# Self-attention key scores without mask matmuls: GpSimd zeroes the unseen exponentials, two score steps are interleaved, value products run two groups behind

## The reference

```python
w = jnp.einsum('bhqd,bhkd->bhqk', q, k) / jnp.sqrt(jnp.asarray(HD, q.dtype))
neg = jnp.finfo(w.dtype).min
if causal_bool:                       # self attention
    mask = jnp.tril(jnp.ones((ql, kl), bool))
    w = jnp.where(mask[None, None], w, neg)
if tril_diag2_additive:               # cross attention
    cm = jnp.tril(jnp.ones((ql, kl), w.dtype), k=2)
    w = w + jnp.where(cm == 0, neg, jnp.zeros((), w.dtype))[None, None]
w = jax.nn.softmax(w, axis=-1)
return jnp.einsum('bhqk,bhkd->bhqd', w, v)
```

## Time and profile before

| | |
|---|---|
| Median of three runs | 1644.99 us |
| Profiled execution | 1647.01 us, its span 1645.3 us |
| PE matmuls busy | 1434.1 us (87%) |
| DVE busy | 1116.3 us (68%) |
| ACT busy | 987.8 us (60%) |
| GpSimd (POOL) busy | 317.8 us (19%) |
| Self phases with both kinds of scores | 16, first to last step 19.58 us in most of them |
| Cross phases with both kinds | 14, first to last step 22.08 to 23.37 us in most of them |

### The profile page before, as it was taken

How to read it: one execution, slowest core, us unless ns; L and a number is a source line. 1 busy time by engine, 2 the same in 40 slices (tenths; PEclk the granted TensorE clock), 3 DMA queues, 4 the chain that set the end, 5 groups by cost and what they waited for, 6 DMA issues and landing times. The chain is left out here.

```text
span 1645.3 us, 39092 instructions
## 1 busy us (share of the span) xinstructions
PE 1434.1 (87%) x15448; PEld 877.4 (53%) x15448; DVE 1116.3 (68%) x3252; ACT 987.8 (60%) x1618; POOL 317.8 (19%) x428
## 2 busy tenths in 40 slices
PE   2667789989898989989898998989899898989887
PEld 1445564655555565655556465555646565555443
DVE  5557676767777776776777676677767667647344
ACT  2255675766757576675757576575757666571642
...
GB/s 69 57 77 52 55 22 55 21 44 38 22 59 9 67 15 39 36 32 50 10 72 10 50 26 39 43 16 64 10 56 20 44 32 28 9 24 12 15 5 9
DMA packets 79214, 58.05 MB, mean 35 GB/s; under 512 B 11004, under 2 KB 78902, under 8 KB 79030
## 3 DMA queue, kind: packets, MB, share of 16 engines
...
...
## 5 line engine op out<-in xcount | busy, mean ns | idle before, releaser
L1025 DVE TENSOR_REDUCE chunkmax<-ps 128x3 f32<-128x384 f32 (+1 forms) x1024 | 508.6, 553 | 119.2 <-PE ps L1379 113.6
L711 ACT ACTIVATE probs<-ps 128x768 f32<-128x768 f32 (+1 forms) x512 | 406.0, 809 | 199.3 <-PE ps L1374 195.5
L1444 PE MATMUL ps<-zT,w 128*128 128x512 f32 x576 | 281.0, 602 | 6.5 <-ACT silu_a L728 4.8
L728 ACT ACTIVATE silu_a<-ps,b 128x512 f32<-128x512 f32 x144 | 98.7, 685 | 197.9 <-PE ps L1444 174.5
L1359 PE MATMUL ps<-k_op,q_op 48*128 48x256 bf16 x512 | 147.4, 290 | 64.4 <-DVE chunkmax L1025 50.8
L1166 DVE SCALAR_TENSOR_TENSOR h_open<-ps,b,silu_a 128x512 f32<-128x512 f32 x128 | 95.8, 749 | 123.6 <-PE ps L1444 111.3
L1444 PEld LDWEIGHTS ps<-zT,w 128*128 128x128 f32 x576 | 102.8, 191 | 114.6 <-issue 87.4
L1341 PE MATMUL ps<-q_op,k_op 51*128 51x256 bf16 x512 | 141.7, 277 | 25.2 <-POOL lower L499 9.3
L1480 PE MATMUL ps<-hT,w 128*128 128x512 f32 x288 | 149.3, 599 | 3.8 <-DVE hT L1172 3.0
L1359 PE MATMUL ps<-xk_op,xq_op 51*128 51x256 bf16 x512 | 143.5, 282 | 6.1 <-DVE chunkmax L1025 5.7
L1371 PE MATMUL ps<-mask_q_lo,ident_lo 64*128 64x256 bf16 x512 | 145.9, 288 | 0.0
...
## 6 DMA issues: line engine op xcount, KB each, us to landing
q_op<-q_parts SPq DMA_DIRECT2D x192, 64.0 KB
xq_op<-xq_parts SPq DMA_DIRECT2D x192, 64.0 KB
...
```

The source lines that it names most:

```text
L711: act.activation(probs[:, four % 2, 2 * pair:2 * pair + 2, 0:T + a.seen], ps[:, 2 * (1 - g % 2):2 * (1 - g % 2) + 2, 0:T + a.seen], ACT.Ex ...
L1025: dve.tensor_reduce(chunkmax[:, b, at, :], ps[:, MAX_BANK[n], 0:3 * a.seen].rearrange("p (c n) -> p c n", c=3), AX.X, ALU.max).then_inc(a. ...
L1444: pe.matmul(ps[:, bank, :], w, src[:], start=True, stop=True).then_inc(sig.sem, 1)
```

## The change

Six edits, made together:

- The self attention's key scores lose both mask matmuls. The masks `mask_k_lo` and `mask_k_hi` and their making in the set-up go.
- GpSimd zeroes the exponentials of unseen keys instead: `keep_seen`, one `affine_select` of 128 partitions by 512 elements for each exponential, 16 per self phase, in place in `probs`. Value groups of the self attention wait for it (`kept`) and no longer for the exponential.
- A self phase takes two steps at a time (`two_steps`), twelve matmuls in six slots.
- Value products run two groups behind in both phases: value groups 0 to 5 follow the steps of groups 2 to 7, and groups 6 and 7 follow at the end.
- `probs` has three buffers of four heads. To make room, three weight tiles used only in the set-up share memory with `geluT`.
- `MAX_BANK` has three banks for steps 0 to 23, two for 24 to 27, then 4, 6, 7 from step 28 on (by number, so that 28 takes bank 6, 29 bank 7, 30 bank 4, 31 bank 6). The first context copy moves behind exponential 11.

```diff
-        probs = sb("probs", [128, 2, 4, T + XW])
+        probs = sb("probs", [128, 3, 4, T + XW])
...
-        MAX_BANK = [(6, 7, 5)[n % 3] for n in range(20)] + [(6, 7)[n % 2] for n in range(20, 24)] \
-            + [(4, 6, 7)[n % 3] for n in range(24, 2 * H)]
+        MAX_BANK = [(6, 7, 5)[n % 3] for n in range(24)] + [(6, 7)[n % 2] for n in range(24, 28)] \
+            + [(4, 6, 7)[n % 3] for n in range(28, 2 * H)]
...
             def other_masks():
-                for m in (mask_k_lo, mask_k_hi, xmask_q_lo, xmask_q_hi, xmask_k_lo, xmask_k_hi, pick):
+                for m in (xmask_q_lo, xmask_q_hi, xmask_k_lo, xmask_k_hi, pick):
                     fill(m[:], 0.0)
...
                 for p in (slice(0, HALF), slice(HALF, 2 * HALF)):
-                    select(mask_k_lo[p], ALU.is_ge, MASKED, 0, [[0, 2], [1, 64]], -1)
-                    select(mask_k_hi[p], ALU.is_ge, MASKED, -HALF, [[0, 2], [1, 128]], -1)
...
+            def keep_seen(a, j, first, last):
+                for g in range(first, last):
+                    four, pair = divmod(g, 2)
+                    late_and_early = probs[:, four % 3, 2 * pair:2 * pair + 2, 0:2 * a.seen]
+                    pool.wait_ge(*a.exp.part(j, g + 1))
+                    pool.affine_select(out=late_and_early, in_=late_and_early, compare_op=ALU.is_ge, fill=0.0, base=0,
+                                       pattern=[[0, 2], [2 if a.cross else 0, 2], [1, a.seen]],
+                                       channel_multiplier=-1).then_inc(a.kept.sem, 1)
...
+                if exists(i):
+                    keep_seen(sa, i, 0, 2)
                 if exists(k):
 
                     pool.wait_ge(*n_mlp.out.done(k))
                     add_bias(h2b, h2, bmlp, ca.h.done(k), h3_sb.before(k), h2b_ready)
+                if exists(i):
+                    keep_seen(sa, i, 2, H)
...
-                    act.wait_ge(*(a.pv.part(j, four - 1) if four >= 2 else used_before))
+                    act.wait_ge(*(a.pv.part(j, four - 2) if four >= 3 else used_before))
...
-                    if g == 10:
+                    if g == 11:
                         context_copy(a, 0, j)
...
+            def second_keys(a, j, par, m):
+
+                kt, qt, h2, k0, q0 = key_operands(a, par, m)
+                last = pe.matmul(bank_of(m)[:, 0:a.seen], kt[:, h2, k0 + 128:k0 + T], qt[:, h2, q0 + T - a.seen:q0 + T],
+                                 start=False, stop=a.selects, skip_group_check=True)
+                if a.selects and m % 2:
+                    last.then_inc(a.st_ps.sem, 1)
...
+            def two_steps(a, j, par, other, jo, paro, n, free_4, free_5):
+
+                first_keys(a, j, par, n)
+                late_queries(a, j, other, jo, paro, n, free_4, free_5)
+                second_keys(a, j, par, n)
+                early_queries(other, paro, n)
+                late_queries(a, j, other, jo, paro, n + 1, free_4, free_5)
+                late_query_mask(other, n)
+                early_queries(other, paro, n + 1)
+                early_query_mask(other, n)
+                first_keys(a, j, par, n + 1)
+                late_query_mask(other, n + 1)
+                second_keys(a, j, par, n + 1)
+                early_query_mask(other, n + 1)
...
-                pe.wait_ge(*a.exp.part(j, 2 * four + 2))
+                pe.wait_ge(*(a.kept if a.selects else a.exp).part(j, 2 * four + 2))
...
-                        score_step(a, j, par, step, other, jo, paro, step, free_4, free_5)
-                    if exists(j) and four:
-                        if four == 1:
+                        if exists(j, jo) and a.selects:
+                            if step % 2 == 0:
+                                two_steps(a, j, par, other, jo, paro, step, free_4, free_5)
+                        else:
+                            score_step(a, j, par, step, other, jo, paro, step, free_4, free_5)
+                    if exists(j) and four >= 2:
+                        if four == 2:
                             free_4()
-                        if four == 5:
+                        if four == 6:
                             free_5()
...
-                        value_group(a, four - 1, j, par)
+                        value_group(a, four - 2, j, par)
                 if exists(j):
+                    value_group(a, 6, j, par)
                     value_group(a, 7, j, par)
```

125 lines of the change are left out of this document (71 added, 54 removed).

## The result

The changed kernel takes 1674.01 us, the median of four runs (1671.0 to 1675.94); the kernel before took 1645.62 in the same comparison (four runs, 1643.63 to 1648.78). The ratio is 1.0168 with a 95% interval of 1.0148 to 1.0188: slower by 28.4 us. The prediction was 1658 us, slower by 13, with a range up to 1668. The sign was right, the size was not. The profiled execution took 1671.0 us (span 1669.2), 24.0 us more than the one before.

A forecast was written before the change was run, and what follows sets the result against it. A loop over three query banks with a value group in line, not PE's slots, was taken to set the self phase's pace. Self phases +9.9, set-up -2.5 and clock +5.6 gave +13.0 us: 1658 us, range 1644 to 1668.

The forecast's parts named there:

- The loop: Middle of a self phase: PE and DVE stay at 2.40 us per group of four steps, 2.88 with two banks.
- the select's length: GpSimd, 512 elements: 632 ns, from a line between two measured rows; range 402 to 1093 ns.
- The price of a self phase: End of each self phase: PE goes on 0.65 us later, as value group 7 waits for select 15.
- the claim about the interleaved order: Self phase loop: the work between the wait on DVE and the value group stays 0.44 us; saved slots only lengthen the wait.
- The line of three value groups: End of a self phase: three groups of 0.80 us in line let value group 7 start 0.51 us later at the earliest.
- Set-up: Before the first self phase: GpSimd's chain of constants shortens by 2.56 us and PE waits for nothing else: -2.5 us.
- The bound of -1: Set-up: the saving is only 1 us if a load is late behind GpSimd's constants.
- The first three turns: Self phases of the first two turns, without an MLP norm ahead of exponential 3, cost 0.4 us each; the third 0.65.
- Cross phases: The third value group falls into the wait for exponential 15: 0 us, bounds 0 to 0.3 each.
- The clock: A pause of about 1.6 us before step 10 halves the clock in 5 of 16 self phases, 1.12 us each: +5.6 us.
- The median: The median of the runs was taken 2.0 us below the profiled execution: 1658.0 instead of 1660.0 us.
- slow selects: Rival: selects of 1093 ns end each self phase 0.46 us later than forecast, +7.4 on top, 1665 us; chance 0.08.

The follow-up runs named there:

- run 4: Changed kernel with single steps in its self phases instead of interleaved ones; selects and value products two behind stay; 1663.5 us, ratio 1.0099.
- run 2: Kernel before with only the later value products (two behind, three buffers, new bank table); mask matmuls and single steps stay, no selects; 1659.4 us, ratio 1.0068.
- run 11: Changed kernel's selects and interleaved steps, with `h2b` behind all selects on GpSimd and every value group cut in two; 1643.7 us, ratio 0.9962.
- run 12: Same as run 10, but 14 unread matmuls in place of 18 in the cross phases' pause; 1625.6 us, ratio 0.9859.
- run 1: Changed kernel with value products one group behind again, old bank table and context copy behind exponential 10; 1675.6 us, ratio 1.0178.
- run 3: Changed kernel without GpSimd's selects, so the causal mask of the self attention's value products is left out; 1668.7 us, ratio 1.0128.
- run 5: Changed kernel with single steps, value products one behind, old bank table and `h2b` behind all selects on GpSimd; 1652.5 us, ratio 1.0040.
- run 6: Kernel before (masks on PE, single steps) with every value group cut in two, three buffers and another bank table; 1651.3 us, ratio 1.0014.
- run 8: Same as run 3, plus ten matmuls that nothing reads, ahead of step 10 of each self phase; 1665.4 us, ratio 1.0080.
- run 10: Selects, single steps, split value groups, last self pair masked on PE, plus 18 unread matmuls ahead of step 19 of cross phases; 1630.7 us, ratio 0.9879.

## Why the prediction was wrong

The measured 1674.0 us lie 16 us above the forecast. The steady self phases account for 2.0 of them, the first three self phases for 4.3, the cross phases for 4.3 and the set-up for 2.0; half clock in the steady self phases took 1.1 less than forecast and the end 0.7 less, and 5.0 come from the place of the profiled execution among the runs. The mechanism that failed is the order of the interleaved steps; by size, the terms for the first turns and for the cross phases weigh more.

**The loop, the select's length: right.** Groups 2.40 us apart and 2.95 with two banks, DVE idle 0.36; selects of 0.642 us where 0.632 was read off a line between two rows. This also bears out the choice of the second figure of the Trainium skill (GPSIMD Engine Reference, section 7) over the first, by which it would have been some 1.06, an estimate.

**The price of a self phase: 0.65 forecast, 0.80 measured, and composed otherwise.** The failed step is the claim about the interleaved order, that behind the wait "each half of the array still has a 256, a 128, a 256 and a 128 column matmul ahead of the value group", so nothing changes. That count is right for the value group and says nothing of what else stands behind the wait: both key matmuls of the second step, and so the exponential. I let exponential 15 end 0.1 us earlier than before; it ends at 503.30, 21.11 us into the phase, where it was 21.10 before. That is most of the 0.15 between forecast and measured. Single steps show what was to be had: 0.60 us of the 0.80 (run 4). The line of three value groups, sized 0.51, costs 0.30 (run 2); with single steps the selects cost nothing more than that.

**Set-up: -2.5 forecast, -0.5 measured.** The step "PE waits for nothing else there" failed: the maxima's transfer was about as late. The bound of -1 that I named was nearer. Over all the traces this start lies between 74.1 and 76.1 us whatever the masks do, so the term is within the spread.

**The first three turns: +1.45 forecast, +5.8 measured.** Forecast as 0.4, 0.4 and 0.65. With single steps (run 4) the first two are 0.85 and 0.37 us shorter than before. Part of that is the clock: the first self phase begins at half clock, which lasts until 10.8 us into it in the changed kernel, 4.6 before and 5.0 in run 4. Runs 11 and 12, with and without the interleaving (12 has its last pair masked on PE besides), have nearly the same mean clock in their first self phases (0.78 and 0.79), and these are only 0.34 us apart (19.52 and 19.18). How much of the first two terms is the order and how much the clock stays open. The second and the third also had more half clock: in the stretch from the self phase to the next phase the mean clock is 0.86 and 0.82, against 0.94 and 0.95 before. In runs 1 to 6 the third is 1.0 to 1.9 us longer than before; why the clock stays down so long there was not settled.

**Cross phases: 0 forecast, +4.3 measured.** At full clock they are 0.18 us longer, 2.5 us in 14: ACT does its context copy behind exponential 11, waits there for value group 3 (on PE from 727.18), and everything behind it is that much later. ACT's timeline in the cross phase at 709.84, changed kernel:

```profile
726.52 1.59 ACT L720 ACTIVATE probs<-ps 128x772 f32<-128x772 f32 x2 [0.80 <-PE ps L1371]
728.17 0.60 ACT L730 ACTIVATE ctx_fm<-ps 128x512 f32<-128x512 f32 x1
728.66 1.64 ACT L698 ACTIVATE z_tm<-xn,tiny_z 128x128 f32<-128x128 f32 x4
```

and in the one at 697.09 of the kernel before:

```profile
715.74 1.63 ACT L689 ACTIVATE z_tm<-xn,tiny_z 128x128 f32<-128x128 f32 x4
```

The norm `z_tm` starts 728.66 - 709.84 = 18.82 us into the phase, before 715.74 - 697.09 = 18.65. With value products one behind it is gone (22.31 in run 5). I had looked only at the third value group. The rest is clock, in two ways. Five of the 11 cross phases are longer by half clock where seven were, but each by 1.3 to 1.5 us instead of 1.0 to 1.3. And four more have a stretch at half clock of 3.4 us that begins 8.0 to 8.5 us into the phase and costs only 0.1 to 0.2: the pause before step 19 then shrinks from 1.94 to 0.60 us and takes it up. Such a stretch stands behind a pause 7.7 us into the phase that is 0.81 us in the kernel before and 1.28 in all traces with value products two behind. Both pauses in the cross phase at 421.65, and that phase:

```profile
429.33 0.28 PE L1393 MATMUL ps<-k_op,q_op 48*128 48x256 bf16 x1 [1.28 <-DVE chunkmax L1034]
...
436.28 0.28 PE L1393 MATMUL ps<-k_op,q_op 48*128 48x256 bf16 x1 [0.60 <-DVE chunkmax L1034]
```

```profile
421.65:444.25 22.60, 19.44 (x333) 13.08 (x334) 18.92 (x64) 17.34 (x31) 8.68 (x12) 0.92 0.04 13
```

So what a stretch at half clock costs depends on the wait behind it: the same 3.4 us cost 0.1 here and 1.45 at 516.52.

**The clock: +5.6 forecast, +4.5 measured in self phases.** Right in kind; near in size partly by luck, since three phases of 13 had it and not five of 16, and one of the three, with two stretches in a row, is 2.24 us longer. The pause is 1.18 us, not 1.6, as PE also waits for DVE in the steps ahead of it (0.19 to 0.48 us, three times). Over all the traces, half clock made 1 to 11 of the 13 steady self phases longer in each of the five kernels with a pause of 1.08 to 1.25 us in these phases (changed, runs 2 to 4 before step 10, run 1 before value group 1), and none in the others, whose longest pause there is 0.65. But "in cross phases I expect as many as before" treats the two as independent. Runs 3 and 8 show that they are not: self 11 and cross 2 of 11, then 0 and 8. The Trainium skill (TensorE: Matmul & The Clock Gate, "HAM oscillation") tells of waits for transfers between bursts of matmuls, some 3 to 5 us long, that put the clock down again and again, and of a loop order without them as the cure. Runs 8, 10 and 12 agree that closing a pause keeps the clock up behind it; they close it by filling it, and their pauses are shorter, 1.2 to 1.6 us.

**The median.** I took 2.0 us off for the profiled execution's place among the runs. It was the fastest of the four after the change, and the median is 3.0 us above it: 5 of the 16 us between 1658 and 1674.

**The range** went up to slow selects and no further. Nothing in it stood for an order of instructions that makes exponentials later, nor for the first turns, and for the cross phases nothing although their bounds of 0 to 0.3 each were named.
